# Count matrix of a graph network in groups of 16 target nodes instead of 8

## The chip, the cores and the metric

The kernel runs on one core of one Trainium2 chip. The metric is device microseconds of one execution, as the median of several runs; less is better. The engines are TensorE (PE; PEld is its weight load), VectorE (DVE), ScalarE (ACT), GpSimd (POOL) and SyncE (SP). Each has a sequencer of its own that fetches, waits, loads registers and issues; instructions of a sequencer carry a q in the rows (PEldq, ACTq).

## What is computed

Four graph layers with residual and layer norm run over 3125 nodes of 64 features and 100000 edges, sorted by target. The stage that matters here serves the first of them, four steps of normalised message passing:

```
for _ in range(num_steps):
    w = _gcn_norm(row, col, n_nodes, x.dtype)
    msgs = w[:, None] * x[row]
    x = jax.ops.segment_sum(msgs, col, num_segments=n_nodes)
```

The kernel does not gather and scatter for this layer. It first builds the dense matrix of counts, `m[source, target]` = number of edges between the two (rows in 25 blocks of 128 source nodes, 3136 columns of target nodes), and then multiplies with it four times.

## The kernel before

**How a count matrix comes out of products.** Edges are held in 782 tiles of 128, sorted by target. Target nodes are taken in groups of GD = 8, so 391 groups. A **step** is one tile of edges against one group. For a step TensorE multiplies two one-hots over the 128 edges of the tile: `lows` (128 edges x 128, the low seven bits of the source) as stationary operand, and `cells` (128 edges x KW = 25 x 8 = 200, the block of the source and the node within the group) as moving one. The product is a 128 x 200 block of counts, added into a bank of PSUM that belongs to the group. A tile on the border of two groups takes part in a step of either; the loop runs over NS = 1184 steps.

**The tables** (`step_tables`, L572 to L618, about 150 to 197 us of the span). VectorE compares step numbers with the first and last step of each tile (`begun` L580, `entered` L581, `chosen` L587), TensorE spreads the edges' keys to their steps in four quarters (L632, L634), and VectorE takes them out (L601 to L608). On one partition L611 to L618 work out the bank of each step (`step_regs`, with the group of a round's last step plus one as its last number) and the step at which each group ends (`group_ends`).

**The stage** (`build_pairs`) runs five programs beside each other:
- vector (L694 to L697): for each **round** of SG = 8 steps it makes the 8 `lows` (L695) and the 8 `cells` (L696) in one of two sets. It waits until the round that used the set before is through (`stepped`).
- tensor (L707 to L717): two rounds to a turn of a loop. For each round its sequencer loads nine numbers of `step_regs` into registers in one instruction (reported as L755, the helper's line), checks the last of them (L711), waits for `emptied` (L712, L713) and for `made` (L714, L715), and issues eight products (L717), each with a small register operation for the bank's address.
- scalar (L732 to L744): for each group in turn it waits for the group's last step, copies half of the sums to the columns of `m` (L726) and clears the bank (L728). Eight banks form a ring. It loads eight counts at once (L751), 24 groups to a turn.
- gpsimd: places edges for a later layer in DRAM by indirect transfers (L445), four to each turn of the vector program's loop (`turned`).
- sync: brings batches for these and clears rows of a DRAM table (`spread`, L502).

All five meet in a barrier at the end of the stage; the matrix is then stored and read again by the multiplications.

The lines of the tensor program's round, since a sentence can't say them:

```
*regs, least = load_values(nc, mybir.EngineType.PE, K.step_regs[0:1, bass.ds(i * 2 + s, 1), 0:SG + 1]..., 0, (SG - 1) * 512)
least = nc.s_assert_within(least, 1, GROUPS)
e.wait_ge(emptied, least)
e.sem_inc(l.sink, 1)
e.wait_ge(made, i * 4 + (s + 1) * 2)
e.sem_inc(l.sink, 1)
for k in range(SG):
    e.matmul(banks[:, bass.ds(regs[k], KW)], lows[s][:, :, k], cells[s][:, k, :], ...).then_inc(stepped, 1)
```

Of the kernel before, what the change touches and what calls it, by code (L numbers as in the profile page):

```python
# [12 lines left out]
P = 128  # L13
NB = 25
NP = NB * P
PW = 24 * P + 64
# [9 lines left out]
BODY = 64  # L26
SG = 8
GD = 8
GROUPS = N // GD + 1
ROUNDS = 148  # L30
NS = ROUNDS * SG
KW = NB * GD
PART = NS // 4
AHEAD = 2 * SG
BIG = 3.0e38
# [132 lines left out]
def fresh(name):  # L168

    _used[name] = _used.get(name, 0) + 1  # L170
    return f"{name}_{_used[name]}"
# [341 lines left out]
def step_tables(nc, K, outer, src, dst):  # L513
# [5 lines left out]
    with Scope(nc) as st:  # L519
# [46 lines left out]
        def vector(l):  # L566
# [4 lines left out]
            v.wait_ge(loaded, 144)  # L571
            v.tensor_scalar(group_i[:, :, :], raw[1][:, :, :], 3, None, ALU.logical_shift_right).then_inc(l.sem, l.add(1))  # L572
            v.tensor_scalar(before_g[:, :], before_i[:, :], 3, None, ALU.logical_shift_right).then_inc(l.sem, l.add(1))
            v.wait_ge(l.sem, l.done())
# [37 lines left out]
            v.wait_ge(l.sem, l.done())  # L612
            v.tensor_scalar(ring_i[:, :], at_i[:, :], SG - 1, None, ALU.bitwise_and).then_inc(l.sem, l.add(1))
            v.tensor_scalar(K.step_regs[:, :, SG:SG + 1], at_i[:, :].rearrange("o (r k) -> o r k", k=SG)[:, :, SG - 1:SG], 1.0, None, ALU.add).then_inc(l.sem, l.add(1))
# [37 lines left out]
def build_pairs(nc, K, m):  # L652
# [3 lines left out]
    with Scope(nc) as st:  # L656
        sb = lambda n, s, d: st.enter_context(nc.sbuf_tensor(fresh(n), s, d))
        sem = lambda n: st.sem(fresh(n))
        cells = [sb(f"step_cells{s}", [P, SG, KW], F16) for s in range(2)]
        lows = [sb(f"step_lows{s}", [P, P, SG], F16) for s in range(2)]  # L660
        row = sb("cell_row", [P, KW], F32)
        row16 = sb("cell_row16", [P, KW], F16)
        rows16 = sb("low_rows16", [P, P, SG], F16)
        none = sb("none16", [P, KW], F16)
        ring = st.enter_context(nc.psum_tensor(fresh("ring"), [P, SG, 512], F32))
        counted, clean, made, stepped, emptied, turned = (sem(n) for n in ("counted", "clean", "made", "stepped", "emptied", "turned2"))

        def gpsimd(l):
            l.eng.iota(row[:, :], pattern=[[1, KW]], base=0, channel_multiplier=0, allow_small_or_imprecise_dtypes=True).then_inc(counted, 1)
            place_batches(l, K, 0, 8, turned, 4)  # L670

# [6 lines left out]
        def vector(l):  # L678
            v = l.eng
            v.sem_inc(stepped, AHEAD)  # L680
            v.memset(none[:, :], 0.0).then_inc(clean, 1)
            v.memset(m[:, :, GROUPS * GD:PW], 0.0).then_inc(l.sem, l.add(1))
            v.wait_ge(counted, 1)
            v.tensor_copy(row16[:, :], row[:, :]).then_inc(l.sem, l.add(1))
            v.tensor_copy(rows16[:, :, :], row[:, 0:P].unsqueeze(2).to_broadcast([P, P, SG])).then_inc(l.sem, l.add(1))

            v.wait_ge(l.sem, l.done())
            pairs = row16[:, :].rearrange("p (w two) -> p w two", two=2).unsqueeze(1).to_broadcast([P, SG, KW // 2, 2])
            with l.loop(ROUNDS // 2) as i:
                for s in range(2):  # L690
                    keys = one_of(K.step_keys, i * 2 + s)
                    cell = keys[:, 0:2 * SG].rearrange("p (k two) -> p k two", two=2).unsqueeze(2).to_broadcast([P, SG, KW // 2, 2])
                    low = keys[:, 2 * SG:3 * SG].unsqueeze(1).to_broadcast([P, P, SG])
                    v.wait_ge(stepped, i * (2 * SG) + (s + 1) * SG)  # L694
                    v.tensor_tensor(lows[s][:, :, :], rows16[:, :, :], low, ALU.is_equal).then_inc(made, 1)  # L695
                    v.tensor_tensor(cells[s][:, :, :].rearrange("p k (w two) -> p k w two", two=2), pairs, cell, ALU.is_equal).then_inc(made, 1)  # L696
                v.sem_inc(turned, 1)  # L697
            v.wait_ge(made, 2 * ROUNDS)

        def tensor(l):  # L700
            e = l.eng
            e.wait_ge(clean, 1)
            e.sem_inc(l.sink, 1)
            for b in range(SG):
                e.matmul(ring[:, b, 0:KW], none[:, 0:P], none[:, :], start=True, stop=False, skip_group_check=True)
            banks = ring[:, :, :].rearrange("p b c -> p (b c)")
            with l.loop(ROUNDS // 2) as i:  # L707
                for s in range(2):
                    *regs, least = load_values(nc, mybir.EngineType.PE, K.step_regs[0:1, bass.ds(i * 2 + s, 1), 0:SG + 1].rearrange("p o k -> p (o k)"),
                                               0, (SG - 1) * 512)  # L710
                    least = nc.s_assert_within(least, 1, GROUPS)  # L711
                    e.wait_ge(emptied, least)  # L712
                    e.sem_inc(l.sink, 1)  # L713
                    e.wait_ge(made, i * 4 + (s + 1) * 2)  # L714
                    e.sem_inc(l.sink, 1)  # L715
                    for k in range(SG):
                        e.matmul(banks[:, bass.ds(regs[k], KW)], lows[s][:, :, k], cells[s][:, k, :],  # L717
                                 start=False, stop=False, skip_group_check=True).then_inc(stepped, 1)

        def scalar(l):  # L720
            a = l.eng
            a.sem_inc(emptied, SG)

            def empty(bank, column):
                sums = ring[:, bank, 0:KW]
                a.activation(m[:, :, column], sums.rearrange("p (h d) -> p h d", d=GD), ACT.Copy, scale=0.5).then_inc(l.sem, l.add(1))  # L726
                a.wait_ge(l.sem, l.done())
                a.activation(sums, sums, ACT.Copy, scale=0.0).then_inc(emptied, 1)  # L728
            turn = 3 * SG
            with l.loop(GROUPS // turn) as i:  # L730
                for c in range(0, turn, SG):
                    over = load_counts(nc, mybir.EngineType.Activation, K.group_ends[0:1, bass.ds(i * turn + c, SG)], NS + AHEAD)  # L732
                    for b in range(SG):
                        a.wait_ge(stepped, over[b])
                        empty(b, bass.ds(i * (turn * GD) + (c + b) * GD, GD))
            assert GROUPS - GROUPS // turn * turn < SG
            over = load_counts(nc, mybir.EngineType.Activation, K.group_ends[0:1, GROUPS // SG * SG:GROUPS], NS + AHEAD)
            for g in range(GROUPS // SG * SG, GROUPS):
                if g < GROUPS - 1:
                    a.wait_ge(stepped, over[g % SG])  # L740
                else:
                    a.wait_ge(stepped, NS + AHEAD)
                empty(g % SG, slice(g * GD, g * GD + GD))
            a.wait_ge(emptied, GROUPS + SG)  # L744
        drive(nc, "build", dict(sync=sync, gpsimd=gpsimd, vector=vector, tensor=tensor, scalar=scalar))


# [1981 lines left out]
```

## Time and profile before

| | |
|---|---|
| median of 3 runs | 5718.8 us (5718.3 to 5719.78) |
| the profiled execution's own time | 5712.27 us |
| its span | 5710.5 us |
| mean granted clock of TensorE | 0.634 of full speed |
| TensorE busy, weight load busy | 2917.1 us (51%), 2314.5 us (41%) |
| VectorE busy | 3715.3 us (65%) |
| ScalarE busy | 1759.2 us (31%) |
| GpSimd busy | 3453.4 us (60%) |

The shares are averages over many stages that come one after the other. The stage of the change is a small part of the span, and the views of the trace can be cut to it: a window gives a stretch in us from the span's start, a line of the source gives its instructions, the sequencer's too, with shortest, median and longest duration.

### The profile page before, as it was taken

Reading aid. Unit: us, or ns where it says so; the run is one execution under the profiler, and the core shown is the slowest. Engines: PE = TensorE matmul, PEld = TensorE weight load, DVE = VectorE, ACT = ScalarE, POOL = GpSimd, SP = SyncE. Lnnn points to the kernel's source line nnn. Section 1 sums busy time; section 2 is a strip of 40 time slices with the busy share of each in tenths; the row PEclk is TensorE's granted clock in tenths of the full one; section 3 lists DMA queues with packets and bytes.
Section 4 is the critical chain, followed back from the end, with each engine's and each line's share of the span. In section 5 each row is a group of like instructions: output and inputs, shape, how many; then the busy total and the mean of one; then the engine's idle time right before and its main releaser. Section 6 shows DMA issues by size and latency. Waiting matters only on the chain. (4 is left out here: it accounts for less than half of the span.)

```text
span 5710.5 us, 76336 instructions
## 1 busy us (share of the span) xinstructions
PE 2917.1 (51%) x18212; PEld 2314.5 (41%) x18213; DVE 3715.3 (65%) x6539; ACT 1759.2 (31%) x5177; POOL 3453.4 (60%) x3383
## 2 busy tenths in 40 slices
PE   4344578724555555264736426455564244555543
PEld 1233456514454444143424225444453234444443
DVE  4645554306777777233332569899998579998987
ACT  0055500001111111110010035655654146556552
POOL 4077337737777777432613477777772577777771
PEclk7655589956666666566857655556655556665655
DMA  6031040027777777500000212222220321222211
GB/s 214 31 106 52 0 142 2 2 79 205 217 214 221 214 216 203 173 9 0 4 7 9 53 42 58 45 54 50 50 46 7 68 54 44 55 49 50 53 32 18
DMA packets 491952, 449.20 MB, mean 79 GB/s; under 512 B 135374, under 2 KB 439172, under 8 KB 491667
## 3 DMA queue, kind: packets, MB, share of 16 engines
q1 hardware_dynamic: 257963, 232.05, 14.7%
q0 software_dynamic: 116768, 136.51, 10.3%
q10 hardware_dynamic: 116936, 77.08, 4.2%
q8 instruction: 149, 2.44, 0.2%
q14 instruction: 136, 1.11, 0.1%
HBM read 308.22 MB, written 137.16 MB: 78 GB/s over the span
## 5 line engine op out<-in xcount | busy, mean ns | idle before, releaser
L2158 POOL DMA_INDIRECT tg<-tab_d,tail_ids x1632 | 1699.1, 1041 | 543.3 <-issue 494.6
L445 POOL DMA_INDIRECT sorted_edges_d<-place_batch x784 | 807.9, 1030 | 749.6 <-DMA place_batch<-place_queue_d 340.0
L2197 PE MATMUL acc<-msg,sum_hot 128*96 128x65 f32 x3264 | 547.0, 366 | 961.0 <-ACT msg L2271 748.5
L2197 PEld LDWEIGHTS acc<-msg,sum_hot 128*96 128x96 f32 x3264 | 529.4, 279 | 976.9 <-issue 976.9
L1494 POOL DMA_INDIRECT xg<-tab_d,src_i x784 | 767.7, 979 | 252.3 <-issue 238.5
L2187 PE MATMUL hr<-near_table,near_hot 128*128 x4896 | 679.2, 266 | 197.2 <-DVE near_hot L2319 95.0
L2187 PEld LDWEIGHTS hr<-near_table,near_hot 128*128 128x128 f16 x4896 | 497.4, 105 | 380.5 <-issue 281.8
L2246 ACT ACTIVATE pr<-hr 128x396 f32<-128x396 f32 x576 | 277.8, 483 | 590.9 <-PE hr L2187 584.7
L2260 ACT ACTIVATE msg<-tg,coef_b 128x64 f32<-128x64 f32 x1632 | 396.6, 334 | 31.3 <-DVEq L2667 31.3
L1508 PE MATMUL hq<-ex,sameU 128*128 128x128 f32 x1568 | 269.2, 350 | 260.5 <-DVEq L1613 194.4
L2487 DVE TENSOR_REDUCE scal<-prod 128x17 f32<-128x1088 f32 x288 | 370.5, 1286 | 9.9
L1508 PEld LDWEIGHTS hq<-ex,sameU 128*128 128x128 f32 x1568 | 262.3, 265 | 275.8 <-issue 275.8
L2266 ACT ACTIVATE pr<-pr,coef_c 128x64 f32<-128x64 f32 x1496 | 365.4, 334 | 0.0
L717 PE MATMUL ring<-step_cells,step_lows 128*128 128x200 f16 x1184 | 229.6, 374 | 232.3 <-DVE step_lows L695 95.6
L906 PE MATMUL aggps<-shared,pair_m 128*128 128x192 bf16 (+1 forms) x1800 | 263.0, 286 | 80.4 <-DVEq L934 65.8
L717 PEld LDWEIGHTS ring<-step_cells,step_lows 128*128 128x128 f16 x1184 | 174.9, 157 | 287.0 <-issue 286.2
L2311 DVE TENSOR_TENSOR scal<-scal 128x68 f32<-128x68 f32 (+1 forms) x1272 | 264.3, 245 | 28.2 <-ACT scal L2251 9.3
L1611 DVE TENSOR_TENSOR h<-hq,xg 128x1792 f32<-128x1792 f32 x56 | 113.4, 2025 | 212.2 <-DMA xg<-tab_d,src_i 206.8
L695 DVE TENSOR_TENSOR step_lows<-low_rows,room 128x1024 f16<-128x1024 f16 x148 | 102.6, 693 | 222.5 <-PE ring L717 222.1
L906 PEld LDWEIGHTS aggps<-shared,pair_m 128*128 (+1 forms) x1800 | 176.1, 99 | 167.3 <-issue 97.5
L1546 ACT ACTIVATE back<-bk 128x896 f32<-128x896 f32 x112 | 102.8, 918 | 443.2 <-PE bk L1518 443.2
L2311 DVE TENSOR_TENSOR prod<-pr,tg 128x1088 f32<-128x1088 f32 x96 | 124.3, 1295 | 169.4 <-DMA tg<-tab_d,tail_ids 166.5
(469 smaller groups left out, 5402.5 us busy)
## 6 DMA issues: line engine op xcount, KB each, us to landing
ex<-spread_d SPq DMA_DIRECT2D x112, 448.0 KB, 5.5
msg_d<-back ACTq DMA_DIRECT2D x112, 448.0 KB
near_hot<-head_row_d SPq DMA_DIRECT2D x96, 408.0 KB
tg<-tab_d,tail_ids POOLq DMA_INDIRECT x1632
spread_d<-zeros ACTq DMA_DIRECT2D x28, 896.0 KB, 10.9
spread_d<-zeros SPq DMA_DIRECT2D x28, 896.0 KB, 8.8
idsU<-dst_short_d SPq DMA_DIRECT2D x112, 224.0 KB, 6.6
pairs_d<-pair_m SPq DMA_DIRECT2D x3, 4800.0 KB
```

The lines of the kernel that those rows point to most:

```text
L445: l.eng.indirect_dma_start(K.sorted_edges[:, :], bass.IndirectOffsetOnAxis(ap=K.batch[:, n % 2, 0, k:k + 1], axis=0), K.batch[:, n % 2, 1, ...
L717: e.matmul(banks[:, bass.ds(regs[k], KW)], lows[s][:, :, k], cells[s][:, k, :], start=False, stop=False, skip_group_check=True).then_inc(s ...
L906: ins = l.eng.matmul(ps[s][:, 0:3 * w], self.m[:, b, bass.ds(at, P)], parts[:, b, :], start=b == 0, stop=b == NB - 1)
L1494: l.eng.indirect_dma_start(xg[j.c % ROWS][:, half * H + k, :], None, K.tab1, bass.IndirectOffsetOnAxis(ap=src_i[:, t:t + 1], axis=0)).then ...
L1508: ins = e.matmul(hq[:, k, :], same[j.slot][:, k, :], ex[j.slot][:, k, :], start=True, stop=True)
L2158: e.indirect_dma_start(tg[:, u % TAILS * GQ + k, :], None, K.tab3, bass.IndirectOffsetOnAxis(ap=K.tail_ids[:, u * GQ + k:u * GQ + k + 1], ...
L2187: ins = e.matmul(hr[(u * FILLS + g) % 2][:, c:c + PW3], near_hot[u % HOTS][:, k, :], rows[:, bass.ds(at[k] + n * PW3, PW3)], start=n == 0, ...
L2197: ins = e.matmul(sums[:, bass.ds(at[k], D + 1)], sum_hot[u % 2][:, k, :], msg[u % QN][:, k, :], start=False, stop=False, skip_group_check= ...
L2260: a.activation(msg[u % QN][:, k, 0:D], tg[:, tails(u).start + k, 0:D], ACT.Copy, scale=kB[s][:, t.start + k:t.start + k + 1]).then_inc(tai ...
L2266: a.activation(r, r, ACT.Copy, scale=kC[s][:, k:k + 1]).then_inc(kinds_scaled, 1)
L2311: tt_ = lambda o, x, y, op: v.tensor_tensor(o, x, y, op).then_inc(l.sem, l.add(1))
L2487: v.tensor_reduce(sc[:, n, q * GQ:(q + 1) * GQ], prod[q % 2][:, :, :], AX.X, ADD).then_inc(l.sem, l.add(1))
```

## The change

Groups of 16 target nodes instead of 8 (GD), hence 196 groups instead of 391, and products of KW = 25 x 16 = 400 columns instead of 200. Rounds of four steps instead of eight (SG), 252 rounds instead of 148, so 1008 steps instead of 1184. Three sets of one-hots instead of two (SETS), so three rounds to a turn of the loops, 84 turns instead of 74. The ring stays at eight banks, which had been as many as steps in a round and now has a name of its own (RING). GpSimd does three transfers to a turn instead of four.

```
-SG = 8
-GD = 8
+SG = 4
+GD = 16
+RING = 8
+SETS = 3
 GROUPS = N // GD + 1
-ROUNDS = 148
+ROUNDS = 252
 NS = ROUNDS * SG
 KW = NB * GD
 PART = NS // 4
-AHEAD = 2 * SG
+AHEAD = SETS * SG
...
-            v.tensor_scalar(group_i[:, :, :], raw[1][:, :, :], 3, None, ALU.logical_shift_right).then_inc(l.sem, l.add(1))
+            v.tensor_scalar(group_i[:, :, :], raw[1][:, :, :], 4, None, ALU.logical_shift_right).then_inc(l.sem, l.add(1))
...
-        cells = [sb(f"step_cells{s}", [P, SG, KW], F16) for s in range(2)]
-        lows = [sb(f"step_lows{s}", [P, P, SG], F16) for s in range(2)]
+        cells = [sb(f"step_cells{s}", [P, SG, KW], F16) for s in range(SETS)]
+        lows = [sb(f"step_lows{s}", [P, P, SG], F16) for s in range(SETS)]
...
-        ring = st.enter_context(nc.psum_tensor(fresh("ring"), [P, SG, 512], F32))
+        ring = st.enter_context(nc.psum_tensor(fresh("ring"), [P, RING, 512], F32))
...
-            place_batches(l, K, 0, 8, turned, 4)
+            place_batches(l, K, 0, 8, turned, 3)
...
-            v.memset(m[:, :, GROUPS * GD:PW], 0.0).then_inc(l.sem, l.add(1))
+            assert GROUPS * GD == PW
...
-            with l.loop(ROUNDS // 2) as i:
-                for s in range(2):
-                    keys = one_of(K.step_keys, i * 2 + s)
+            with l.loop(ROUNDS // SETS) as i:
+                for s in range(SETS):
+                    keys = one_of(K.step_keys, i * SETS + s)
...
-                    v.wait_ge(stepped, i * (2 * SG) + (s + 1) * SG)
+                    v.wait_ge(stepped, i * (SETS * SG) + (s + 1) * SG)
...
-            for b in range(SG):
+            for b in range(RING):
                 e.matmul(ring[:, b, 0:KW], none[:, 0:P], none[:, :], start=True, stop=False, skip_group_check=True)
...
-            with l.loop(ROUNDS // 2) as i:
-                for s in range(2):
-                    *regs, least = load_values(nc, mybir.EngineType.PE, K.step_regs[0:1, bass.ds(i * 2 + s, 1), 0:SG + 1].rearrange("p o k -> p (o k)"),
-                                               0, (SG - 1) * 512)
+            with l.loop(ROUNDS // SETS) as i:
+                for s in range(SETS):
+                    *regs, least = load_values(nc, mybir.EngineType.PE, K.step_regs[0:1, bass.ds(i * SETS + s, 1), 0:SG + 1].rearrange("p o k -> p (o k)"),
+                                               0, (RING - 1) * 512)
...
-                    e.wait_ge(made, i * 4 + (s + 1) * 2)
+                    e.wait_ge(made, i * (2 * SETS) + (s + 1) * 2)
...
-            a.sem_inc(emptied, SG)
+            a.sem_inc(emptied, RING)
...
-            turn = 3 * SG
+            turn = 3 * RING
```

## Rows read from the trace of the kernel before

**Rows 1.** The page: the span.
```profile
span 5710.5 us, 76336 instructions
```

**Rows 2.** Products of L717, 276 to 741 us: durations ns min/median/max, first and last start.
```profile
L717 PE MATMUL ring<-step_cells,step_lows x1184: 371/371/391, 278.1 to 738.0; 128*128 128x200 f16 x198
```

**Rows 3.** In order of time, behind the stage: start us, us, engine line what.
```profile
740.36 8.36 SPq L1072 DMA_DIRECT2D pairs_d<-pair_m  x2
```

**Rows 4.** Groups by line, 278 to 739.7 us: count, busy us, mean ns, idle before, releasers.
```profile
L445 POOL DMA_INDIRECT sorted_edges_d<-place_batch x224 | 262.0, 1170 | 91.2 <-issue 67.3 <-DVEq L697 21.5 <-DMA place_batch<-place_queue_d 2.4
L717 PE MATMUL ring<-step_cells,step_lows 128*128 128x200 f16 x1184 | 229.6, 374 | 232.3 <-DVE step_lows L695 95.6 <-ACT ring L728 94.2 <-issue 36.8
...
L696 DVE TENSOR_TENSOR step_cells<-cell_row,room 128x1600 f16<-128x1600 f16 x147 | 144.8, 985 | 0.0
L726 ACT ACTIVATE pair_m<-ring 128x200 f32 (+1 forms) x391 | 130.5, 334 | 154.2 <-PE ring L717 153.4
L728 ACT ACTIVATE ring<-ring 128x200 f32<-128x200 f32 x391 | 125.9, 322 | 12.3
L695 DVE TENSOR_TENSOR step_lows<-low_rows,room 128x1024 f16<-128x1024 f16 x147 | 101.9, 693 | 222.1 <-PE ring L717 222.1
L726 ACT ACT_TABLE_LOAD x16 | 20.5, 1283 | 318.8 <-PE ring L717 315.7 <-issue 3.1
```

**Rows 5.** TensorE in order of time: rounds of eight products.
```profile
545.40 1.56 PE L717 MATMUL ring<-step_cells,step_lows 128*128 128x200 f16 x8 [1.68 <-DVE step_lows L695]
...
657.45 1.55 PE L717 MATMUL ring<-step_cells,step_lows 128*128 128x200 f16 x8 [1.67 <-ACT ring L728]
660.12 1.55 PE L717 MATMUL ring<-step_cells,step_lows 128*128 128x200 f16 x8 [1.12 <-ACT ring L728]
663.35 1.55 PE L717 MATMUL ring<-step_cells,step_lows 128*128 128x200 f16 x8 [1.67 <-DVE step_lows L695]
666.02 1.55 PE L717 MATMUL ring<-step_cells,step_lows 128*128 128x200 f16 x8 [1.13 <-DVE step_lows L695]
...
734.10 1.56 PE L717 MATMUL ring<-step_cells,step_lows 128*128 128x200 f16 x8 [1.68 <-DVE step_lows L695]
```

**Rows 6.** VectorE and ScalarE in order of time beside these rounds.
```profile
661.84 0.69 DVE L695 TENSOR_TENSOR step_lows<-low_rows,room 128x1024 f16<-128x1024 f16 x1 [1.08 <-PE ring L717]
661.93 0.32 ACT L728 ACTIVATE ring<-ring 128x200 f32<-128x200 f32 x1
662.45 0.98 DVE L696 TENSOR_TENSOR step_cells<-cell_row,room 128x1600 f16<-128x1600 f16 x1
...
663.86 0.34 ACT L726 ACTIVATE pair_m<-ring 128x200 f32 x1 [1.60 <-PE ring L717]
```

**Rows 7.** Sequencer of TensorE by line, windows of 664 to 667 us; ns, first and last start.
```profile
L755 PEldq TENSOR_LOAD <-room x1: 847/847/847, 664.3 to 664.3; - x1
...
L711 PEldq FUSED_REGOPS  x1: 151/151/151, 665.2 to 665.2; - x1
L711 PEldq SEQ_ASSERT  x1: 18/18/18, 665.5 to 665.5; - x1
...
L713 PEldq EVENT_SEMAPHORE  x1: 51/51/51, 665.5 to 665.5; - x1
...
L715 PEldq EVENT_SEMAPHORE  x1: 51/51/51, 665.8 to 665.8; - x1
...
L717 PEldq FUSED_REGOPS  x8: 37/37/37, 665.9 to 666.7; - x8
...
L89 PEldq EVENT_SEMAPHORE  x1: 51/51/51, 666.9 to 666.9; - x1
```

**Rows 8.** Register loads: of 17 and 9 numbers (PE), 8 and 7 (ACT).
```profile
L755 PEldq TENSOR_LOAD <-regs x192: 1353/3712/4235, 3239.8 to 5655.4; - x192
L755 PEldq TENSOR_LOAD <-room x148: 841/848/2835, 275.2 to 735.1; - x148
...
L751 ACTq TENSOR_LOAD <-room x21: 545/549/551, 542.1 to 718.7; - x21
...
L751 ACTq TENSOR_LOAD <-room x1: 989/989/989, 727.4 to 727.4; - x1
```

**Rows 9.** In order of time: SyncE clears rows of the spread table.
```profile
322.56 3.54 SPq L502 DMA_DIRECT2D spread_d<-zeros  x4
```

**Rows 10.** The register load by line, 322 to 335 us.
```profile
L755 PEldq TENSOR_LOAD <-room x3: 1339/2623/2754, 323.7 to 333.3; - x3
```

**Rows 11.** Window 660 to 740 us: busy us of each engine, granted clock, DMA share.
```profile
660.00:740.00 80.00, 41.90 (x216) 31.91 (x216) 40.62 (x51) 44.22 (x142) 0.00 (x0) 0.50 0.00 0
```

**Rows 12.** The page, costliest groups: a ScalarE copy of 396 columns.
```profile
L2246 ACT ACTIVATE pr<-hr 128x396 f32<-128x396 f32 x576 | 277.8, 483 | 590.9 <-PE hr L2187 584.7
```

**Rows 13.** Indirect transfers of GpSimd by line, 276 to 741 us.
```profile
L445 POOL DMA_INDIRECT sorted_edges_d<-place_batch x224: 954/962/1752, 277.3 to 626.5; - x112
```

**Rows 14.** The tables, in order of time.
```profile
154.38 0.53 DVE L580 TENSOR_SCALAR begun<-steps,last_step 112x1184 f16<-112x1184 f16 x1
154.83 0.32 DVE L581 TENSOR_SCALAR entered<-steps,first_group 112x392 f16<-112x392 f16 x1
155.06 0.52 DVE L580 TENSOR_SCALAR begun<-steps,last_step 112x1184 f16<-112x1184 f16 x1
...
160.80 9.63 DVE L587 SCALAR_TENSOR_TENSOR chosen<-steps,first_step,begun 112x1184 f16<-112x1184 f16 x7
...
179.82 1.05 PE L632 MATMUL stepps<-chosen,cell 112*128 112x296 f16 x7
...
183.54 1.05 PE L632 MATMUL stepps<-chosen,cell 112*128 112x296 f16 x7
...
193.68 0.77 DVE L611 TENSOR_SCALAR group_ati<-group_at 1x1184 int32<-1x1184 f32 x1
194.47 0.76 DVE L613 TENSOR_SCALAR ring_i<-group_ati 1x1184 int32<-1x1184 int32 x1
...
195.48 0.76 DVE L616 TENSOR_SCALAR room<-ring_i 1x1184 int32<-1x1184 int32 x1
196.17 0.55 DVE L618 SCALAR_TENSOR_TENSOR room<-stepps,count_f 1x392 int32<-1x392 f32 x1
```

More of the change, by code:

```diff
@@ L571, in vector @@
             v.wait_ge(loaded, 144)
-            v.tensor_scalar(group_i[:, :, :], raw[1][:, :, :], 3, None, ALU.logical_shift_right).then_inc(l.sem, l.add(1))
-            v.tensor_scalar(before_g[:, :], before_i[:, :], 3, None, ALU.logical_shift_right).then_inc(l.sem, l.add(1))
+            v.tensor_scalar(group_i[:, :, :], raw[1][:, :, :], 4, None, ALU.logical_shift_right).then_inc(l.sem, l.add(1))
+            v.tensor_scalar(before_g[:, :], before_i[:, :], 4, None, ALU.logical_shift_right).then_inc(l.sem, l.add(1))
             v.wait_ge(l.sem, l.done())
@@ L612, in vector @@
             v.wait_ge(l.sem, l.done())
-            v.tensor_scalar(ring_i[:, :], at_i[:, :], SG - 1, None, ALU.bitwise_and).then_inc(l.sem, l.add(1))
+            v.tensor_scalar(ring_i[:, :], at_i[:, :], RING - 1, None, ALU.bitwise_and).then_inc(l.sem, l.add(1))
             v.tensor_scalar(K.step_regs[:, :, SG:SG + 1], at_i[:, :].rearrange("o (r k) -> o r k", k=SG)[:, :, SG - 1:SG], 1.0, None, ALU.add).then_inc(l.sem, l.add(1))
@@ L728, in empty @@
                 a.activation(sums, sums, ACT.Copy, scale=0.0).then_inc(emptied, 1)
-            turn = 3 * SG
+            turn = 3 * RING
             with l.loop(GROUPS // turn) as i:
-                for c in range(0, turn, SG):
-                    over = load_counts(nc, mybir.EngineType.Activation, K.group_ends[0:1, bass.ds(i * turn + c, SG)], NS + AHEAD)
-                    for b in range(SG):
+                for c in range(0, turn, RING):
+                    over = load_counts(nc, mybir.EngineType.Activation, K.group_ends[0:1, bass.ds(i * turn + c, RING)], NS + AHEAD)
+                    for b in range(RING):
                         a.wait_ge(stepped, over[b])
                         empty(b, bass.ds(i * (turn * GD) + (c + b) * GD, GD))
-            assert GROUPS - GROUPS // turn * turn < SG
-            over = load_counts(nc, mybir.EngineType.Activation, K.group_ends[0:1, GROUPS // SG * SG:GROUPS], NS + AHEAD)
-            for g in range(GROUPS // SG * SG, GROUPS):
+            assert GROUPS - GROUPS // turn * turn < RING
+            over = load_counts(nc, mybir.EngineType.Activation, K.group_ends[0:1, GROUPS // RING * RING:GROUPS], NS + AHEAD)
+            for g in range(GROUPS // RING * RING, GROUPS):
                 if g < GROUPS - 1:
-                    a.wait_ge(stepped, over[g % SG])
+                    a.wait_ge(stepped, over[g % RING])
                 else:
                     a.wait_ge(stepped, NS + AHEAD)
-                empty(g % SG, slice(g * GD, g * GD + GD))
-            a.wait_ge(emptied, GROUPS + SG)
+                empty(g % RING, slice(g * GD, g * GD + GD))
+            a.wait_ge(emptied, GROUPS + RING)
         drive(nc, "build", dict(sync=sync, gpsimd=gpsimd, vector=vector, tensor=tensor, scalar=scalar))
```

## The prediction, made before the changed kernel ran

> **What bounds the kernel now.** The page gives the whole, and the products by line give the place of the change: the count matrix is built by one stage, whose products run from 278.1 us to the end of the last product at 738.0 + 0.37 = 738.4 us, so some 460 us of a span of 5710.5 [rows 1, 2]. A stage ends behind all engines and the next one starts after it (the transfer of `pair_m` at 740.36 [rows 3]), so what this stage gains or loses, the kernel gains or loses.
>
> Next I read busy time in the stage: TensorE 229.6 us, VectorE 144.8 + 101.9, ScalarE 130.5 + 125.9 + 20.5, GpSimd 262.0 [rows 4]. No engine is busy much over half of the 460 us. So I looked for the rhythm. In order of time the rounds of eight products start at 657.45, 660.12, 663.35, 666.02: steps of 2.67 and 3.23 in turn, and 545.40 to 734.10 holds 32 turns of the loop, 5.897 us each [rows 5]. That regularity speaks for an engine that waits for nobody. The view blames "ACT ring" or "DVE step_lows" for the 1.1 and 1.7 us before each round, but the rows of those engines deny it: the set that VectorE finishes at 662.45 + 0.98 = 663.43 is for the round of 666.02, and ScalarE's last emptying before the round of 663.35 ended at 661.93 + 0.32 = 662.25, 1.1 us before it [rows 6].
>
> The idle time is TensorE's own sequencer. Its instructions do not count as busy but can be asked for by line [rows 7]: eight small register operations of L717 begin between 665.9 and 666.7, and the loop's end (L89) comes at 666.9, so eight products are issued in 0.93 us, 0.116 each (by the tenths printed, 0.10 to 0.13). For the round before, the register load of L755 starts at 664.3, takes 0.847 and is done at 665.2; L711 (0.151 and 0.018), L713 (0.051), L714, L715 (0.051) follow, and the first product is issued at 665.9. A round is 8 x 0.116 = 0.93 of issue, 0.85 of load and 0.89 of the rest, together 2.67; the loop's turn costs 5.897 - 2 x 2.67 = 0.557 more. The array streams eight products in about 1.55 us and idles 1.12 [rows 5].
>
> **What the change does to this.** Per round the sequencer issues 4 products instead of 8, and loads 5 numbers instead of 9. Everything else of the round stays: L711 to L715, the two waits, the address arithmetic. There are 252 rounds instead of 148, in 84 turns of three instead of 74 turns of two.
>
> Issue: 4 x 0.116 = 0.464 less per round.
>
> Load: the trace has no load of 5. It has 9 numbers in 0.847 [rows 7], 17 numbers in 1.353 at the least, 8 numbers (on ScalarE) in 0.549, and 7 numbers (ScalarE again) in 0.989 [rows 8]. From 9 to 17 a number costs (1.353 - 0.847) / 8 = 0.063, which gives 0.847 - 4 x 0.063 = 0.595 for 5. But 7 cost more than 8, so odd counts seem to be taken in pieces, and 5 is odd too: I take 0.65. The ends are 0.35 (5/8 of the 0.549, if 5 go as smoothly as 8) and 0.99 (the row of 7).
> The Trainium skill ("DMA: Bandwidth & Descriptors", Latency and other measured facts) gives a tensor load a floor of about 600 ns. The 0.549 row is already below that figure; by the figure as a price for 5 the stage would end about 13 us sooner than I say, and the sum does not use it.
>
> A round without the turn is then 2.67 - 0.464 - (0.847 - 0.65) = 2.01 us. A turn of three is 3 x 2.01 + 0.557 = 6.59. I leave the turn's price as it is; the number of a round is now i x 3 + s where it was i x 2 + s, same forms.
>
> **Sum of the loop.** Before: 74 x 5.897 = 436.4. After: 84 x 6.59 = 553.6. Difference **+117**. Rounds are what costs: 104 more of them, each carrying 1.5 us that has nothing to do with the products.
>
> **Stalls.** The stage takes 460 us, not 436.4; the rest, some 24 us, lies in loads that last up to 2.835 instead of 0.848 [rows 8] while SyncE clears the spread rows (four transfers from 322.56 on): in that stretch of 13 us three loads took 1.339, 2.623 and 2.754 [rows 9, 10]. The transfers stay the same in number and size. Rounds are nearer together, so a stretch catches perhaps 2.3 loads where it caught 2: +3 us. If a shorter load is also held up less, this is -8; if more loads are caught, +8.
>
> **What does not bind.** The array: 4 products of 400 columns. 8 of 200 go in 1.55 us including the last one's 0.371, that is 0.168 each at the half clock (granted 0.50 in 660:740, the 1.2 GHz level [rows 11]); 4 of 400 then stream in 4 x 0.337 = 1.35, under 2.01. Should the busier array be granted 2.4 GHz, nothing is gained, since it waits for issue anyway.
> VectorE: 1024 elements in 693 ns and 1600 in 985 [rows 4] make 0.507 ns an element and 174 fixed; 512 elements cost about 0.43. The second one-hot keeps 1600 elements (4 x 400 for 8 x 200). A pair now takes 1.6 (661.84 to 663.43 [rows 6]); then 1.34, under 2.01. The third set gives it more lead, which nobody needs.
> ScalarE: 200 columns cost 0.334 and 0.322 [rows 4], 396 columns 0.483 [rows 12], so emptying a group grows from 0.60 to about 0.92 us, but there are 196 instead of 391; 180 us in all, beside 580. The wait for an emptied bank looks eight groups back, now about ten rounds. After the last product one longer emptying sticks out: +0.3.
> GpSimd: 224 indirect transfers, now three to a turn of 6.59; at 962 ns [rows 13] and 67.3 / 224 = 0.3 of issue between them [rows 4] they need 3.8. They end with turn 75 of 84, so still within the stage. The last one began at 626.5 before.
>
> **The tables before it.** 1008 steps instead of 1184, 197 group columns instead of 392. L587 costs 9.63 / 7 = 1.376 for 1184 columns, nearly all per element: 15% less is -1.4. L580 and L581 start 0.67 apart as a pair and carry (0.53 - 0.32) / (1184 - 392) = 0.27 ns a column: 7 x (176 + 195) x 0.27 = -0.7. The quarters follow each other by 3.72 us (179.82, 183.54), 28 products of 296 columns, now 252: 15% of 3.5 quarters, -1.9. The one-partition rows L611, L613, L616, L618: -0.5 [rows 14]. Together **-4.5**.
> Setting up the stage: eight clearing products of 400 columns instead of 200 (+1.3 at most), a smaller constant at L685 (-0.3): between 0 and +1, taken as 0.
>
> **Total:** 117 + 3 + 0.3 - 4.5 = +116. The profiled execution took 5712.3 us (span 5710.5); it becomes 5828. The median of the runs shown is 5718.8, 6.5 above the profiled one, so I forecast **5835**.
>
> **Rivals.**
> A, the other side: the round's fixed part hides under the long products, and the count of steps decides. Then the stage scales with steps, 460 x 1008 / 1184 = 392, -68, and the time is 5718.8 - 68 - 4.5 = 5646. It decides from the point where a turn of three takes under 436.4 / 84 = 5.20 us, so a round under 1.55, which needs a load of 5 numbers in 0.19 us. Against it: the load already starts (664.3) before the array is done and still the array idles; what could be hidden is hidden. For it: only that 5 numbers are unmeasured. Chance 0.03.
> The Trainium skill ("TensorE: Matmul & The Clock Gate", Specifications table and the queue depths of Part 1) gives TensorE a queue of 64 instructions, by which the sequencer could run far ahead of products of 400 columns. The trace agrees that it runs ahead, but 1.12 us of idle array per round say that issue, not the queue, is short; by that rule alone the stage would come to 252 x 1.35 = 340 us.
> B: the load does not shrink with its count, 0.85 to 0.99. +50 to +86 over the forecast: 5885 to 5920. The 0.989 row for 7 numbers speaks for it, the 1.353 for 17 against. Chance 0.12.
> C: VectorE becomes the bound, because its operands now run four elements deep instead of eight and lose their rate. At twice the per-element cost for both one-hots a pair takes 0.69 + 1.80 - 0.16 = 2.3 against 2.01, about 252 x 2.33 = 587 instead of 554: 5870. The one-hot of L696 keeps its inner pairs and its rate, so little speaks for it. Chance 0.04.
> D: the load is short, 0.35 to 0.5: 252 x 0.15 to 0.30 less, 5760 to 5797. The 0.549 row for 8 speaks for it. Chance 0.14.
> Forecast as told (load 0.5 to 0.85): 0.67, 5797 to 5885.
>
> **Range:** the forecast's own span with most of B's and D's nearer halves: 5780 to 5890. About 0.2% (11 us) is what a measurement of this kernel can tell from no change. Every case but A is slower by more than that; for A and what I have not thought of: faster 0.03, same 0.02, slower 0.95.
>
> **What would show it.** Right: rounds of four products alternate by about 2.0, 2.0, 2.57 us; the load of L755 lasts 0.5 to 0.85, 252 times; L711 to L715 keep their durations; VectorE and ScalarE idle more than half the stage; the stage lasts some 575 to 580 us; everything behind it is shifted and otherwise unchanged. Wrong: rounds under 1.6 us apart (A); a load above 0.85 (B); L695 and L696 back to back with TensorE behind them (C). If the stage is as I say and the total is not, a later stage has moved, which no row here prepares.

## The result

| | before | changed |
|---|---|---|
| median of 3 runs | 5718.8 us | 5816.8 us (5806.3 to 5819.0) |
| profiled execution | 5712.3 us | 5819.0 us |
| its span | 5710.5 us | 5817.2 us |

The changed kernel is slower: ratio 1.0174, 95% interval 1.0161 to 1.0188. A second set of runs on the same kind of chip gave 5816.5 beside 5717.8, ratio 1.0179 (1.0165 to 1.0193). The forecast was 5835 us, with a range of 5780 to 5890.

Where it lies: the products' stage. First the products by line (duration in ns, first and last start), and the first transfer behind the stage.

```profile
L719 PE MATMUL ring<-step_cells,step_lows x1008: 332/537/542, 272.3 to 834.2; 128*128 128x400 f16 x168
```
```profile
837.43 8.36 SPq L1074 DMA_DIRECT2D pairs_d<-pair_m  x2
```

The products begin 5.8 us sooner than before and take from 272.3 to 834.2 + 0.54 = 834.7, 562.4 us where it was 460.3; the next stage starts at 837.43, not 740.36 [rows 1 to 3]: 97.1 us later. The groups of the stage answer to [rows 4]:

```profile
L719 PE MATMUL ring<-step_cells,step_lows 128*128 128x400 f16 x1008 | 366.1, 514 | 196.3 <-DVE step_lows L697 67.6 <-issue 49.0 <-DVE step_cells L698 45.8
L698 DVE TENSOR_TENSOR step_cells<-cell_row,room 128x1600 f16<-128x1600 f16 x252 | 248.2, 985 | 0.0
L447 POOL DMA_INDIRECT sorted_edges_d<-place_batch x224 | 240.4, 1073 | 257.8 <-DVEq L699 209.3 <-issue 46.5 <-DMA place_batch<-place_queue_d 2.0
L719 PEld LDWEIGHTS ring<-step_cells,step_lows 128*128 128x128 f16 x1008 | 129.9, 129 | 432.3 <-issue 409.9
L697 DVE TENSOR_TENSOR step_lows<-low_rows,room 128x512 f16<-128x512 f16 x251 | 106.8, 426 | 225.0 <-PE ring L719 225.0
L728 ACT ACTIVATE pair_m<-ring 128x400 f32 (+1 forms) x196 | 98.6, 503 | 334.1 <-PE ring L719 326.1 <-issue 7.8
L730 ACT ACTIVATE ring<-ring 128x400 f32<-128x400 f32 x196 | 95.7, 488 | 6.3
```

VectorE is busy 355 of 562 us, ScalarE 205, GpSimd 240: nobody is full, and the weight loads stand idle 410 us "until issue". The rhythm, in order of time (start, length, idle before), answers to [rows 5]:

```profile
700.99 1.52 PE L719 MATMUL ring<-step_cells,step_lows 128*128 128x400 f16 x4 [0.97 <-DVE step_lows L697]
702.95 1.52 PE L719 MATMUL ring<-step_cells,step_lows 128*128 128x400 f16 x4 [0.44 <-issue]
704.91 1.52 PE L719 MATMUL ring<-step_cells,step_lows 128*128 128x400 f16 x4 [0.44 <-issue]
707.41 1.52 PE L719 MATMUL ring<-step_cells,step_lows 128*128 128x400 f16 x4 [0.98 <-DVE step_lows L697]
...
739.49 1.52 PE L719 MATMUL ring<-step_cells,step_lows 128*128 128x400 f16 x4 [0.98 <-DVE step_lows L697]
```

Rounds start 1.96, 1.96 and 2.50 us apart; six turns from 700.99 to 739.49 make 6.417 each. And here is the sequencer's load, which answers to the second line of [rows 8]; the second line here is ScalarE's load of four numbers:

```profile
L757 PEldq TENSOR_LOAD <-room x252: 582/593/1965, 270.0 to 831.8; - x126
```
```profile
L753 ACTq TENSOR_LOAD <-room x1: 314/314/314, 810.0 to 810.0; - x1
```

The sequencer's own rows beside these rounds, 540 to 740 us, answer to [rows 7] (L713 is the check, L715 and L717 the two waits):

```profile
L713 PEldq FUSED_REGOPS  x92: 151/151/151, 540.1 to 738.7; - x92
L715 PEldq EVENT_SEMAPHORE  x92: 51/51/51, 540.4 to 739.0; - x92
L717 PEldq EVENT_SEMAPHORE  x92: 51/51/51, 540.7 to 739.2; - x92
```

The waiting itself would stand as a gap before such a row (in e7, where VectorE does hold TensorE up, it is above 0.1 us in 57 of 124 rounds, up to 1.55). Over the whole stage that gap is at most 0.062 us before either wait in the kernel before (148 rounds), and in the changed kernel it is above 0.12 us once before each (0.15 and 0.20 us, of 252). So what the two waits ask for has happened before the sequencer asks.

84 x 6.417 = 539.0 us of loop, 102.6 more than the 436.4 of before; 23.4 us of stalls beside 23.9; a start 5.8 sooner; 0.7 more between the last product and the next stage. 102.6 - 0.5 - 5.8 + 0.7 = 97.0, the 97.1 that the transfer's start shows.

### The profile page after: what moved, and what is told of

Its sections match the earlier page's. It is cut to its first block and busy times, and to the rows that moved or that the text cites. A ratio compares the mean times of both kernels' runs of the same rounds, so it can differ in the third digit from the quotient of the medians.

```text
span 5817.2 us, 75900 instructions
## 1 busy us (share of the span) xinstructions
PE 3058.5 (53%) x18036; PEld 2278.0 (39%) x18037; DVE 3811.3 (66%) x6746; ACT 1709.1 (29%) x4779; POOL 3439.0 (59%) x3383
## 5 line engine op out<-in xcount | busy, mean ns | idle before, releaser
L447 POOL DMA_INDIRECT sorted_edges_d<-place_batch x784 | 785.9, 1002 | 877.1 <-DMA place_batch<-place_queue_d 296.8
L719 PE MATMUL ring<-step_cells,step_lows 128*128 128x400 f16 x1008 | 366.1, 514 | 196.3 <-DVE step_lows L697 67.6
L719 PEld LDWEIGHTS ring<-step_cells,step_lows 128*128 128x128 f16 x1008 | 129.9, 129 | 432.3 <-issue 409.9
L697 DVE TENSOR_TENSOR step_lows<-low_rows,room 128x512 f16<-128x512 f16 x252 | 107.3, 426 | 225.4 <-PE ring L719 225.0
L698 DVE TENSOR_TENSOR step_cells<-cell_row,room 128x1600 f16<-128x1600 f16 x252 | 248.2, 985 | 0.0
```

What stands on the lines that cost most here:

```text
L447: l.eng.indirect_dma_start(K.sorted_edges[:, :], bass.IndirectOffsetOnAxis(ap=K.batch[:, n % 2, 0, k:k + 1], axis=0), K.batch[:, n % 2, 1, ...
```

## The experiments

e1 to e4 ran on a second chip, and e1 again, e8 and e9 on a third. There the kernel before takes 7542 and 7558 us. In the stretches that move most data, the pages of these kernels show about 150 to 165 GB/s where the changed kernel's first page shows some 215; that this is all of the difference was not tried. The rounds of the products' stage do not feel it (6.42 us a turn in e2 there, 6.417 in the changed kernel), so I read the stage's length from the traces, and times only beside those of the kernel before on the same chip (whose runs scatter by 30 us there). Lengths are from the first product's start to the last one's end.

| kernel | products, us | next stage starts | time against the kernel before |
|---|---|---|---|
| before | 460.3 | 740.4 | |
| changed | 562.4 | 837.4 | +98.0, again +98.8 |
| e1, wide only | 391.0, again 391.2 | 696.2, again 695.4 | -60.5, again -69.8 |
| e2, short rounds only | 665.4 | 945.8 | +194.2 |
| e3, two sets | 581.6 | 857.3 | +104.5 |
| e4, check twice | 606.2 | 882.5 | +129.2 |
| e5, load of eight | 561.3 | 837.4 | +97.2 |
| e6, clears earlier | 537.9 | 877.0 | +136.2 |
| e7, pairs of rounds | 362.4 | 696.2 | -41.3 |
| e8, seven batches | 355.8 | 661.2 | -94.6 |
| e9, load of seven | 688.6 | 966.5 | +207.4 |

On the first kind of chip (the changed kernel, e5 to e7) the last column follows the shift of the one before it within 3 us. On the two slow chips every version comes out 11 to 25 us better against the kernel before than the start of its next stage says (e2: 205 us later, +194; e1: 44 and 45 us sooner, -60 and -70). There is no trace of the kernel before from these chips, so the cause is open, and the argument rests on the first two columns.

**The change's two halves.** e1 keeps the wide groups and undoes the short rounds (to fit in SBUF, four small tiles lie in unused columns of another tile):

```
-SG = 4
+SG = 8
-SETS = 3
+SETS = 2
-ROUNDS = 252
+ROUNDS = 124
-            place_batches(l, K, 0, 8, turned, 3)
+            place_batches(l, K, 0, 8, turned, 4)
```

> Groups of 16 and products of 400 columns as in the changed kernel, but rounds of eight steps and two sets as before: 124 rounds in 62 turns. Theory (TensorE's sequencer sets the pace, per round): a round costs what it cost before, 2.67 us plus 0.557 per turn of two, so the loop takes 62 x 5.9 = 366 us instead of 436.4, the stage some 390 instead of 460, and the kernel about 5645 us, faster than before. The array would stream 8 x 0.333 = 2.67 us a round at the half clock, so it is just covered; a round may come out at 2.7 to 3.0. Rival (the columns are what costs, 992 x 400 against 1184 x 200): the loss of the change stays or grows, 5800 us or more. Second rival (VectorE becomes the bound, a pair of one-hots takes 0.69 + 1.80 - 0.16 = 2.3 us): rounds of 2.3 plus waits, no gain beyond the theory's, its rows would stand back to back.

e2 keeps the short rounds and undoes the wide groups:

```
-GD = 16
+GD = 8
-ROUNDS = 252
+ROUNDS = 300
-            v.tensor_scalar(group_i[:, :, :], raw[1][:, :, :], 4, None, ALU.logical_shift_right)...
+            v.tensor_scalar(group_i[:, :, :], raw[1][:, :, :], 3, None, ALU.logical_shift_right)...
```

> Groups of 8 and products of 200 columns as before, but rounds of four steps and three sets as in the changed kernel: 300 rounds in 100 turns. Theory: the products are half as long and the rounds still start 1.96, 1.96 and 2.50 us apart, 6.41 a turn, 641 us of loop against 436.4, so about 5925 us. Rival (columns cost): 240000 columns as before, so about 5720 us. Rival (the array is the bound in part): rounds shorter than 1.96, between the two.

The rounds of e1, with their granted clock (the column of 1.00 in the window's row), and then those of e2:

```profile
656.89 1.57 PE L720 MATMUL ring<-step_cells,step_lows 128*128 128x400 f16 x8 [1.09 <-DVE step_lows L698]
660.11 1.57 PE L720 MATMUL ring<-step_cells,step_lows 128*128 128x400 f16 x8 [1.65 <-ACT ring L731]
662.78 1.57 PE L720 MATMUL ring<-step_cells,step_lows 128*128 128x400 f16 x8 [1.10 <-issue]
```
```profile
600.00:660.00 60.00, 31.46 (x160) 21.91 (x160) 49.60 (x42) 32.25 (x66) 50.55 (x32) 1.00 0.01 0
```
```profile
426.81 0.85 PE L719 MATMUL ring<-step_cells,step_lows 128*128 128x200 f16 x4 [1.63 <-DVE step_cells L698]
428.79 0.85 PE L719 MATMUL ring<-step_cells,step_lows 128*128 128x200 f16 x4 [1.13 <-DVE step_lows L697]
430.74 0.85 PE L719 MATMUL ring<-step_cells,step_lows 128*128 128x200 f16 x4 [1.10 <-DVE step_cells L698]
433.23 0.86 PE L719 MATMUL ring<-step_cells,step_lows 128*128 128x200 f16 x4 [1.63 <-DVE step_cells L698]
```

e1 has the rounds of the kernel before to the hundredth, 3.22 and 2.67 apart, with products twice as wide. e2 has those of the changed kernel, 1.98, 1.95 and 2.49, with products half as wide; the array idles longer and nothing else happens. e1's 391 us were expected as 390, and e2's 665 are its 641 us of loop and 24 of stalls. So the width of a product costs nothing in these two kernels, the round is what is paid, and the loss of the change is all of its short rounds: they cost 205 us alone, and the wide groups win 69 alone; together they do not add up, because wide groups leave fewer rounds to pay for. In e1 TensorE was at the full 2.4 GHz for most of the stage (835 of its 992 products took about 0.333 us each): eight products of 400 columns in 1.57 us, the time of eight of 200 at 1.2 GHz. By the 0.333 us apart at which the changed kernel's products start, eight of them would stream for 2.67 us at the half clock, just a round (an estimate), so nothing wider would be free there. The next stage of e1 starts at 696.2, 44 us sooner than in the kernel before, though its products end 74 us sooner; what holds it is found at e7.

**The third set.**

```
-SETS = 3
+SETS = 2
-            place_batches(l, K, 0, 8, turned, 3)
+            place_batches(l, K, 0, 8, turned, 2)
```

> The changed kernel with two sets of one-hots and two rounds to a turn instead of three; GpSimd does two transfers a turn. Theory: only the loop's turns grow, 126 instead of 84, each 0.54 us: +23 us over the changed kernel, 5840. Rounds within a turn stay at 1.96 us. Rival (the third set gives VectorE the lead that it needs): rounds get longer by themselves, and VectorE's rows end just before the round that uses them; +50 us or more. Rival (turns cost nothing because they hide behind products of 400 columns): 5817.

Rounds start at 419.94, 421.89, 424.36, 426.32, 428.79: 1.96 within a turn, 2.47 over it. 581.6 us, 19.2 more than with three sets (23 expected), for 42 more turns at about 0.5. The third set gives no lead that anyone uses; it only makes turns fewer. A round in which the clock had risen shows that the clock does not matter either: four products in 0.86 us instead of 1.52, and the next round still 1.96 us later.

```profile
433.22 0.86 PE L719 MATMUL ring<-step_cells,step_lows 128*128 128x400 f16 x4 [0.98 <-ACT ring L730]
435.18 1.28 PE L719 MATMUL ring<-step_cells,step_lows 128*128 128x400 f16 x4 [1.10 <-DVE step_lows L697]
```

**The sequencer's work, doubled at one place.**

```
-                    least = nc.s_assert_within(least, 1, GROUPS)
+                    least = nc.s_assert_within(least, 1, GROUPS + 1)
+                    least = nc.s_assert_within(least, 1, GROUPS)
```

> The changed kernel with the bounds check of the round's last number done twice, so one register operation of about 0.15 us and one assertion more per round, and nothing else. Theory (all of the sequencer's own work is on the path): 0.29 us a round, 252 rounds, +72 us, 5889. If the second check is cheaper than the first (one bound is known), +40 at least. Rival (the sequencer's work hides behind the array, which is busy 1.5 of 1.96 us): within 10 us of the changed kernel, 5817.

The added instructions, by line, and three rounds:

```profile
L714 PEldq ALU_OP  x44: 34/38/41, 700.2 to 799.3; - x44
L714 PEldq SEQ_ASSERT  x44: 18/18/18, 700.3 to 799.4; - x44
```
```profile
421.93 1.52 PE L720 MATMUL ring<-step_cells,step_lows 128*128 128x400 f16 x4 [0.61 <-DVE step_lows L697]
424.05 1.52 PE L720 MATMUL ring<-step_cells,step_lows 128*128 128x400 f16 x4 [0.61 <-DVE step_lows L697]
426.71 1.52 PE L720 MATMUL ring<-step_cells,step_lows 128*128 128x400 f16 x4 [1.14 <-DVE step_lows L697]
```

The second check has one bound left to test and is the cheap case: 0.056 us of instructions. With what lies between them a round grows by 0.17 us, from 1.96 to 2.12 or 2.13. 606.2 - 562.4 = 43.8 us, 252 x 0.174; 72 were forecast, 40 for the cheap case. It shows in full in every round, though the array is busy 1.52 of 1.96 us. That excludes the rival of the hidden sequencer.

**What a register load costs.** In e5 and e9 each round loads eight or seven numbers instead of five; the added ones repeat the fifth and are not used:

```
-            v.tensor_scalar(K.step_regs[:, :, SG:SG + 1], at_i[:, :]...[:, :, SG - 1:SG], 1.0, None, ALU.add)...
+            v.tensor_scalar(K.step_regs[:, :, SG:SG + 4], at_i[:, :]...[:, :, SG - 1:SG].to_broadcast([1, ROUNDS, 4]), 1.0, None, ALU.add)...
...
-                    *regs, least = load_values(... 0:SG + 1] ...)
+                    *regs, least, _, _, _ = load_values(... 0:SG + 4] ...)
```

> The changed kernel, but each round's register load takes eight numbers instead of five (the last three repeat the fifth and are not used). Theory (a load is made in pieces of a power of two, 5 = 4 + 1 takes 0.593 and 7 = 4 + 2 + 1 takes 0.989, 8 in one piece 0.549): the load takes 0.55, a round is 0.04 us shorter, 11 us less than the changed kernel. Rival (a load costs by its count, 0.063 us a number, as 5, 9 and 17 numbers have it: 0.593, 0.848, 1.353): 0.78, a round 0.19 longer, 48 us more.

> The changed kernel with seven numbers in each round's register load instead of five (the last two repeat the fifth and are not used). Eight took the same 0.592 us as five. First theory (blocks of four, a part counts as a whole): 0.59 again, the time of the changed kernel. Second (four at a time, what is left one by one, as 0.989 us for ScalarE's load of seven says): 4 + 1 + 1 + 1, about 1.10, a round 0.5 longer, +128 us. Third (pieces of a power of two, 4 + 2 + 1): 0.85, +64 us.

The loads of e5, then of e9:

```profile
L757 PEldq TENSOR_LOAD <-room x252: 587/592/1989, 271.1 to 831.8; - x126
```
```profile
L757 PEldq TENSOR_LOAD <-room x252: 1057/1069/3737, 270.9 to 960.4; - x126
```

Eight cost the same as five, 0.592, and seven nearly twice as much. e5's stage took 561.3 us beside the changed kernel's 562.4. Both theories of e5 had the size wrong; of those of e9 the second holds. All the durations measured fit one reading: numbers go four at a time, and what is left goes one by one. Counted in such pieces, 4 numbers are one piece (0.314, ScalarE), 5 and 8 are two (0.593, 0.592; ScalarE's 8 0.549), 9 three (0.847), 7 four (1.069; ScalarE 0.989), 17 five (1.353). A piece costs about 0.25, and 0.09 come on top. Two, three and six numbers were not measured. e9's stage took 688.6 us, 126 more than the changed kernel's; 128 were expected.

**The stalls.** The 28 clears that lie beside the products go to the queue and stage of the other 28:

```
-            for n in range(STEPS // 2):
+            for n in range(STEPS):
                 clear_rows(l, K, K.spread1, n)
...
-                for step in range(STEPS // 2 + n * 4, min(STEPS // 2 + n * 4 + 4, STEPS)):
-                    clear_rows(l, K, K.spread1, step)
```

> The changed kernel with the 28 clears of the spread table moved out of the products' stage, to ScalarE's queue of an earlier stage, where the other 28 are. Theory (the stage's 24 us over 84 turns of 6.41 are register loads held up by these transfers): no load over 0.7 us in the stage, which then takes 539 to 542 us instead of 562; what the earlier stages pay is theirs. Rival (the long loads come from the indirect transfers or from elsewhere): the stage stays at 562 and loads of 1.9 us remain.

```profile
L755 PEldq TENSOR_LOAD <-room x252: 583/594/792, 334.0 to 871.3; - x126
```

The longest load is 0.79 instead of 1.97 (0.7 expected), and the stage takes 537.9 us (539 to 542 expected), which is 84 turns of 6.4 and nothing else. So the changed kernel's 23 us of stalls are loads held up by those clears. For the kernel before this was not tried; its long loads lie beside the same clears [rows 9, 10]. The whole kernel gets 37 us slower than the changed one, since the stages before pay 64 (the first product at 336.4 instead of 272.3).

**The changed kernel again.**

> The changed kernel itself once more, beside the kernel before on the same chip. The products' stage should take 562 us as in its first trace, against 460 before, whatever the rest of the kernel takes on this chip. Theory (all of the loss is in this stage, less some 5 us won in the tables): 97 us above the kernel before. Rival (a later stage adds some 10 us of its own, as the first pair of traces shows): 107 us, and the drift between the traces appears again between 1300 and 2300 us.

The stage is 562 us and the next one starts 97.2 us late. By the end of the trace the distance to the kernel before is 103 us, where it was 107 the first time; the medians say 98 and 99. The drift does appear in both traces behind 1300 us, but of a different size, so it stays open whether the later stages lose anything.

**A version that beats both.** e7 is e1 with one register load, one check and one wait for `emptied` for two rounds, and four rounds to a turn:

```
-            with l.loop(ROUNDS // SETS) as i:
-                for s in range(SETS):
-                    *regs, least = load_values(... bass.ds(i * SETS + s, 1), 0:SG + 1] ...)
-                    least = nc.s_assert_within(least, 1, GROUPS)
-                    e.wait_ge(emptied, least)
-                    e.sem_inc(l.sink, 1)
+            with l.loop(ROUNDS // 4) as i:
+                for c in range(4):
+                    s = c % 2
+                    if s == 0:
+                        *regs, least = load_values(... bass.ds(i * 2 + c // 2, 1), 0:2 * SG + 1] ...)
+                        least = nc.s_assert_within(least, 1, GROUPS)
+                        e.wait_ge(emptied, least)
+                        e.sem_inc(l.sink, 1)
...
```

> Groups of 16 and rounds of eight (124 of them, two sets), and besides one register load of 17 numbers, one bounds check and one wait for emptied banks for two rounds, four rounds to a turn. Theory: per two rounds the sequencer needs 16 x 0.115 of issue, 1.353 of load and some 1.1 of the rest, 4.3 us, plus 31 turns of 0.55: 285 us. VectorE's pair of one-hots, 2.33 us, comes level: 124 x 2.33 = 289. So the stage takes some 300 to 315 us with the stalls, against 460 before, and the kernel is 150 us below the kernel before. Rival (the array at the half clock is the bound, 992 x 0.333 = 330 us of streaming, if the clock does not rise): 340 to 360 us. Rival (with two sets VectorE waits for the products and they for it): rounds of 2.33 + 1.6, the stage near 460.

It is faster than the kernel before, 5676.5 beside 5717.8 us, ratio 0.9928 (0.9915 to 0.9942), but the stage is not the 300 to 315 us that I expected. Its rounds in a quiet stretch, a pair at the half clock, and its loads:

```profile
604.87 2.93 PE L722 MATMUL ring<-step_cells,step_lows 128*128 128x400 f16 x16 [2.19 <-issue]
609.38 1.57 PE L722 MATMUL ring<-step_cells,step_lows 128*128 128x400 f16 x8 [1.59 <-DVE step_cells L699]
611.72 1.57 PE L722 MATMUL ring<-step_cells,step_lows 128*128 128x400 f16 x8 [0.76 <-DVE step_cells L699]
615.48 4.59 PE L722 MATMUL ring<-step_cells,step_lows 128*128 128x400 f16 x16 [2.19 <-ACT ring L733]
```
```profile
502.39 5.31 PE L722 MATMUL ring<-step_cells,step_lows 128*128 128x400 f16 x16 [5.27 <-ACT ring L733]
```
```profile
L760 PEldq TENSOR_LOAD <-room x62: 1356/1366/4853, 269.4 to 628.9; - x62
```

Four rounds take 10.6 us (604.87 to 615.48), not 9.2: after the pair that runs through, the next rounds wait for VectorE's `cells`, since with two sets it can begin only when a round is over. 31 such turns are 329 us. Of the other 33 some 20 lie in turns with a held-up load (of five pieces, up to 4.85 us), and most of the rest in turns at the half clock, 11 to 12 us long, in which sixteen products take 5.31 us instead of 2.93. Nine of the 62 loads are held up. In the turn behind such a load about half of the products mostly run at the half clock, but turns without one have such products too (198 of 992 in all). So the rival of the half clock holds in part. My sum had each engine's work but not their turns with two sets.

The stage does not end with the products either. They are over at 636.4, and the next stage starts at 696.2, as in e1. The last of GpSimd's transfers begins at 684.91:

```profile
L447 POOL DMA_INDIRECT sorted_edges_d<-place_batch x224 | 345.3, 1542 | 71.5 <-issue 68.8 <-DMA place_batch<-place_queue_d 2.1 <-DVEq L700 0.6
```
```profile
684.91 0.96 POOL L447 DMA_INDIRECT sorted_edges_d<-place_batch  x1 [0.31 <-issue]
696.18 8.11 SPq L1077 DMA_DIRECT2D pairs_d<-pair_m  x2
```

GpSimd, idle 258 us in the changed kernel (209 of them until VectorE's turns), has next to no such wait left: the products end, and GpSimd goes on sending. The next stage starts 10 us after its last transfer was issued; what fills these 10 us I did not look for. e1 once more, and e8, which moves one batch of transfers out of the stage:

> The kernel with groups of 16 and rounds of eight (124 rounds, two sets) once more, on this chip. In its first trace the products ended 391 us after they began, but the next stage began only when GpSimd had sent its 224 transfers, at 696 instead of 740. Theory (GpSimd is the bound of the stage once the products take under some 420 us): the next stage begins at 696 again, 44 us sooner than in the kernel before, so 40 to 45 us less than the kernel before in all, as the kernel with paired rounds. Rival (paired rounds bring something of their own): this one is 20 to 28 us slower than that one.

```
-            place_batches(l, K, 0, 8, turned, 4)
+            place_batches(l, K, 0, 7, turned, 4)
...
-            for n in range(8):
+            for n in range(7):
                 queue_batches(l, K, n, 1)
...
-                queue_batches(l, self.K, 8, 10)
+                queue_batches(l, self.K, 7, 11)
...
-                place_batches(l, self.K, 8, 10, full[0], 6)
+                place_batches(l, self.K, 7, 11, full[0], 6)
```

> The kernel with paired rounds, but GpSimd sends seven batches of 28 transfers beside the products instead of eight, and eleven instead of ten in the stage behind it, of the four multiplications. Theory (GpSimd bounds the products' stage and, at 1.25 us a transfer, nearly bounds the next one as well): the products' stage ends 28 x 1.65 = 46 us sooner, near 650 us, and the next grows by up to 28 x 1.25 = 35 us, so 10 to 15 us less in all than with eight batches. Rival (the next stage has room for them): 46 us less. Rival (something else than GpSimd ends the products' stage): it still ends at 696.

```profile
661.24 8.17 SPq L1077 DMA_DIRECT2D pairs_d<-pair_m  x2
```

e1 starts its next stage at 695.4, as e7 does, with products that end 30 us later: what they share is GpSimd's work. In time e1 is 69.8 us below the kernel before, where 40 to 45 (or 20 to 28 less than that) were expected; neither theory has it, and it is the open difference of the slow chips. e8 starts its next stage at 661.2, 34 us sooner than e1 on the same chip (its paired rounds had moved nothing of that in e7), so it is GpSimd that ends this stage. 46 us were expected, because I priced the 28 transfers at 1.65 us; but those at the end of the stage, with VectorE through, start 1.26 us apart, and 28 x 1.26 = 35.

e8's four multiplications take 539.6 us (668.0 to 1207.6) where e1's take 525.6: a good half of the gain stays, and its median is 25 us under e1's (10 to 15 expected). Its ratio to the kernel before is 0.988 (0.9863 to 0.9897). It was not run on the first kind of chip, and there it may win nothing: the multiplications of e7 are over at 1073 and GpSimd's last transfer of that stage starts at 1113.62, so this stage ends with GpSimd too, and a batch moved into it would only be paid there.

```profile
L1018 PE MATMUL hopps<-parts_b,pair_m x50: 242/246/246, 890.1 to 1073.0; 128*64 128x192 bf16 x50
```
```profile
1113.62 0.95 POOL L447 DMA_INDIRECT sorted_edges_d<-place_batch  x1 [0.30 <-issue]
```

## Why the prediction was right

**The bound.** Right, and now shown rather than inferred: e4's 0.17 us on the sequencer come out in full, and e1 and e2 keep the round when the product changes. Nobody waits for the "ring" and the "step_lows" that the views name as releasers: the two waits pass at once.

**The issue term.** Right: 0.464 less was forecast. The round went from 2.67 to 1.96, of which 0.847 - 0.593 is the load; 0.456 are left for four products, 0.114 each.

**The load.** The mis-sized term. I took 0.65 for five numbers; it is 0.593. 252 x 0.057 = 14.4 us of the 19 us by which the stage was overrated. The straight line through 9 and 17 numbers had said 0.595, and I left it because of ScalarE's 0.989 for seven. That row was no outlier: it is the price of seven, as e9 shows, but it says nothing about five. The Trainium skill's floor of about 600 ns ("DMA: Bandwidth & Descriptors", Latency and other measured facts) comes near to the 0.593, but ScalarE's load of four took 0.314, so it is no floor.

**The turn.** 0.557 forecast, 0.54 found.

**The stalls.** +3 forecast, -0.5 found: by my count over the trace 23 of 252 loads were held up instead of 16 of 148, each for less. That the clears are their cause was a guess then, and e6 shows it.

**The tables.** -4.5 forecast, the first product comes 5.8 sooner.

**The sum.** +116 forecast, 97.1 in the stage: 14.4 of the load, 3.5 of the stalls and 1.3 of the tables are the difference. The profiled execution ended 106.7 later; the 9.6 beyond the stage were in no term. They halved the error of the profiled execution (5819 where 5828 was forecast), which is luck.

**The rivals.** A (steps decide) falls: the stage went up by 102, and e2 shows 300 rounds costing 205 us more than 148 with nearly equal steps. The Trainium skill's queue of 64 for TensorE ("TensorE: Matmul & The Clock Gate", the table of specifications at its head) does not contradict it: in the kernel before the sequencer starts the next load at 664.3, while the array still streams, and it was still late. B fell with the load at 0.593; but a row of seven numbers would have made it true. C fell: 426 ns for 512 elements, 0.43 forecast, its rate kept. D fell.
What I said would not bind did not, in this kernel: ScalarE 1.0 us a group (0.92 forecast), VectorE and GpSimd idle 225 and 258 us. I had priced GpSimd's transfers at 0.962 us, which is their median in [rows 13]; their mean is 1.170 [rows 4], and 1.073 in the changed kernel, which made no difference here. I had not asked what GpSimd's 224 transfers allow as the stage's least, about 420 us here; that decided e1 and e7.

## What to carry to other kernels

Where no engine is full and the rhythm is exact to the hundredth, the sequencer of the engine that sets the pace is the suspect: list its instructions by line, look for gaps before its waits, and price a loop by its rounds (register load, check, waits, branch) and not by its work. Here larger rounds paid, even with wider products, and so did register loads of four or eight numbers instead of seven. When a stage gets shorter, ask first which of its companions needs the time that you take away.

## What the runs showed of the hardware

The register loads fit four numbers at a time and what is left one by one, about 0.25 us each: 4 numbers 0.31 (ScalarE), 5 and 8 both 0.59, 9 0.85, 7 1.07, 17 1.35. Beside the clears of the spread table a load takes up to three and a half times as long (0.593 to 1.97; 1.37 to 4.85).
Eight products of 400 columns ran at the full 2.4 GHz in the time that eight of 200 took at 1.2 GHz; between rounds the array idled as long in both kernels (1.1 and 1.65 us). The granted clock was 1.00 in that stretch of e1 and 0.50 in the kernel before [rows 11].
GpSimd's indirect transfers took 1.07 us in the mean in the changed kernel, 1.17 in the kernel before and 1.54 in e7, where VectorE is busier. In e7 they take 1.66 in the mean while the products run and 0.96 once these and VectorE's one-hots are over. What slows them was not tried.
